# Query and key rows of an attention layer: turned by VectorE and a way through DRAM instead of by TensorE

## What is computed

```python
x = x + 0.5 * ffn(layernorm(x))
x = x + attn(layernorm(x))
x = x + 0.5 * ffn(layernorm(x))

# attn, 32 query heads, 8 key/value heads, 128 columns a head
q, k, v = x @ Wq.T, x @ Wk.T, x @ Wv.T           # split into heads
q, k = rmsnorm(q, q_norm_w), rmsnorm(k, k_norm_w)
scores = q @ k.T / sqrt(128) + alibi_and_causal_bias
out = softmax(scores) @ v                        # 4 query heads share a key/value head
return out @ Wo.T
```

## Time and profile before

| | us |
|---|---|
| median of 3 runs | 1220.47 (1220.09 to 1221.01) |
| span of the profiled execution | 1218.6 |
| one round of 8 units in attention (slots 29 to 36) | 92.85 |

### The profile page before, as it was taken

One profiled execution on the slowest core, in us unless ns is written; L12 is line 12 of the kernel. 1 busy time (PEld: TensorE's weight loads), 2 busy tenths in 40 slices (PEclk: granted clock), 3 DMA queues, 4 the chain that ended last, 5 costly groups with the idle time before them and its releaser, 6 DMA issues.

```text
span 1218.6 us, 18533 instructions
## 1 busy us (share of the span) xinstructions
PE 1206.2 (99%) x6368; PEld 1062.1 (87%) x6368; DVE 834.9 (69%) x2035; ACT 753.5 (62%) x1758; POOL 652.8 (54%) x526
## 2 busy tenths in 40 slices
PE   6999999999999999999999999999999999999999
PEld 5888888899998999999999999999999888888887
DVE  7876665776666577677677677667767878755555
ACT  4554442357677767767768767767767774544442
POOL 5796561635675625724824824823824343865550
DMA  6152222212213123122122122122122020221101
GB/s 235 42 175 94 103 105 104 94 47 87 79 44 104 44 79 103 39 84 96 44 87 89 50 87 87 53 79 96 53 78 87 20 68 9 71 69 53 52 18 69
DMA packets 33596, 93.77 MB, mean 77 GB/s; under 512 B 4128, under 2 KB 5056, under 8 KB 31456
## 3 DMA queue, kind: packets, MB, share of 16 engines
q1 hardware_dynamic: 33264, 92.29, 22.2%
q10 hardware_dynamic: 240, 0.30, 0.1%
HBM read 62.69 MB, written 29.88 MB: 76 GB/s over the span
## 4 chain that ended last, share of the span: by engine, by line
PE 98%; DVE 1%; DMA 0%; ACT 0%; SPq 0%; issue 0%
PE bank L369 22%; PE bank L367 22%; PE bank L368 21%; PE bank L674 6%; PE bank L479 4%; PE bank L473 4%; PE bank L474 4%; PE bank L688 3%; PE bank L693 3%; PE bank L689 3%; PE bank L619 2%; PE bank L395 1%; PE bank L655 1%; PE bank L622 1%; PE bank L383 1%; DMA x_rows<-x 0%
## 5 line engine op out<-in xcount | busy, mean ns | idle before, releaser
L1066 ACT ACTIVATE prob<-prob,neg_top 128x128 f32<-128x128 f32 (+3 forms) x256 | 141.2, 554 | 87.6 <-DVE neg_top L1517 56.9
L1817 POOL TENSOR_TENSOR rows<-rows,row_root_y 128x640 f32<-128x640 f32 x64 | 80.5, 1257 | 194.1 <-DVE row_root_y L1205 192.9
L1811 POOL TENSOR_TENSOR square<-rows 128x640 f32<-128x640 f32 x64 | 79.3, 1254 | 158.7 <-DVE rows L1560 131.1
L1686 POOL TENSOR_TENSOR w_l_late<-raw_late,w_h_late 128x512 fp32r<-128x512 f32 (+1 forms) x59 | 91.5, 1565 | 71.8 <-ACT w_h_late L809 71.8
L1075 ACT ACTIVATE prob<-prob,inverse 128x128 f32<-128x128 f32 (+3 forms) x252 | 121.1, 553 | 4.4 <-DVE inverse L1522 4.4
L1535 DVE TENSOR_TENSOR probT_l<-bank,probT_h 128x512 fp32r<-128x512 f32 x160 | 101.4, 683 | 28.5 <-ACT probT_h L1081 28.5
L1081 ACT CAST probT_h<-bank 128x512 fp32r<-128x512 f32 x160 | 84.6, 596 | 41.4 <-PE bank L674 41.4
L1281 DVE SCALAR_TENSOR_TENSOR x_rows<-bank,x_rows 128x512 f32<-128x512 f32 x111 | 74.8, 687 | 44.4 <-PE bank L479 44.4
L367 PE MATMUL bank<-o_h,oT_h 128*128 128x512 f32 x256 | 104.7, 409 | 0.0
L369 PE MATMUL bank<-o_h,oT_l 128*128 128x512 f32 x256 | 100.8, 394 | 0.0
L368 PE MATMUL bank<-o_l,oT_h 128*128 128x512 f32 x256 | 99.8, 390 | 0.0
(11 more groups left out here) (237 smaller groups left out, 3808.5 us busy)
## 6 DMA issues: line engine op xcount, KB each, us to landing
x_ring<-x_between SPq DMA_DIRECT2D x64, 256.0 KB, 2.6
x_between<-x_ring SPq DMA_DIRECT2D x56, 256.0 KB, 2.0
raw_late<-w_qkv SPq DMA_DIRECT2D x8, 1536.0 KB, 6.5
raw_early<-ffn_w SPq DMA_DIRECT2D x21, 512.0 KB, 4.1
scaled<-raw_early SPq DMA_DIRECT2D x21, 512.0 KB, 2.7
raw_late<-scaled SPq DMA_DIRECT2D x21, 512.0 KB, 3.7
raw_late<-w_o SPq DMA_DIRECT2D x8, 1024.0 KB, 5.0
x_between<-x_rows SPq DMA_DIRECT2D x8, 256.0 KB, 2.0
```

The source lines that it names most:

```text
L1066: last = act.activation(p, p, ACT.Exp, bias=neg_top[:, h:h + 1], scale=-1.0, accum_out=total[:, h:h + 1])
L1686: return pool.tensor_tensor(lo, raw, hi.bitcast(F32), ALU.subtract)
```

## The change

The rows of 54 units (list BLOCKED: 4 to 60 without 6, 10 and 14) no longer go through TensorE. As soon as GpSimd has normed them, VectorE transposes the 128x640 rows in 32x32 squares, SBUF to SBUF (`block_rows(n + 2)`): in odd slots behind the inversion of the sums (and behind oT_l), in even slots between the ring addition and probT_l. SP stores the squares in DRAM, where there are two rooms, and loads them back by four DMAs that put each square in its place (`store_rows`, `fetch_rows`). ScalarE and VectorE then make rounded parts and remainders from the SBUF tile turned_rows instead of from PSUM. The scale now goes to k instead of q. In the order of SP, the store and the four loads of unit n + 2 stand around ring_store and ring_load of the slot. Scores of such a unit wait for two new semaphores. The room for DMA descriptors of GpSimd is halved, to make room in SBUF.

```diff
+SQ = 32
+BLOCKED = tuple(n for n in range(4, UNITS - 3) if n % TB != 2 or n > 2 * B * TB)
+        row_blocks = sb("row_blocks", [P // SQ, G + 1, SQ])
+        turned_rows = sb("turned_rows", [P // SQ, G + 1, SQ])
+        def by_block(queries):
+            return queries[:, :, :].rearrange("p h (a t) -> p a h t", t=SQ)
@@ tensor: scores
+                if n in BLOCKED:
+                    pe.wait_ge(q_rest_done, blocked_nth(n) + 1)
+                    pe.wait_ge(k_rest_done, blocked_nth(n) + 1)
@@ tensor: slot
-                turn_rows(n + 1)
+                if n + 1 not in BLOCKED:
+                    turn_rows(n + 1)
@@ scalar: turn_rows
+                if n in BLOCKED:
+                    act.wait_ge(rows_back, 16 * (P // SQ) * (blocked_nth(n) + 1))
+                    act.copy(by_block(qT_h), turned_rows[:, :, 0:G, :]).then_inc(qT_hi_done, 1)
+                    act.activation(kT_h[:, t * P:(t + 1) * P].rearrange("p (a q) -> p a q", q=SQ), turned_rows[:, :, G, :], ACT.Copy,
+                                   scale=k_scale[:, g:g + 1]).then_inc(kT_hi_done, 1)
+                    return
@@ vector: turn_rows
+                if n in BLOCKED:
+                    dve.wait_ge(qT_hi_done, n + 1)
+                    dve.tensor_tensor(by_block(qT_l), turned_rows[:, :, 0:G, :], by_block(qT_h).bitcast(F32), ALU.subtract).then_inc(q_rest_done, 1)
+                    cols = slice(t * P, (t + 1) * P)
+                    dve.wait_ge(kT_hi_done, n + 1)
+                    dve.scalar_tensor_tensor(kT_l[:, cols].rearrange("p (a q) -> p a q", q=SQ), turned_rows[:, :, G, :], k_scale[:, g:g + 1],
+                                             kT_h[:, cols].bitcast(F32).rearrange("p (a q) -> p a q", q=SQ),
+                                             ALU.mult, ALU.subtract).then_inc(k_rest_done, 1)
+                    return
@@ vector
+            def block_rows(n):
+                dve.wait_ge(rows_normed, n + 1)
+                if blocked_nth(n):
+                    dve.wait_ge(rows_away, 16 * blocked_nth(n))
+                dve.transpose(row_blocks[:, :, :, :], rows[:, n % LEAD, 0:G + 1, :].rearrange("p h (b k) -> p b h k", k=SQ)).then_inc(rows_blocked, 1)
@@ vector: slot, ahead of turn_rows and add_products
+                if n % 2 and n + 2 in BLOCKED:
+                    block_rows(n + 2)
@@ vector: slot, behind project_out, ahead of turn_probabilities(n)
+                if n % 2 == 0 and n + 2 in BLOCKED:
+                    block_rows(n + 2)
@@ sync
+            def store_rows(n):
+                nth = blocked_nth(n)
+                if nth > 1:
+                    sp.wait_ge(rows_back, 16 * (P // SQ) * (nth - 1))
+                sp.wait_ge(rows_blocked, nth + 1)
+                sp.dma_start(row_turns[nth % 2], row_blocks[:, :, :, :].rearrange("p b h t -> p (b h t)")).then_inc(rows_away, 16)
+            def fetch_rows(n):
+                nth = blocked_nth(n)
+                away = row_turns[nth % 2]
+                if nth:
+                    sp.wait_ge(q_rest_done, nth)
+                    sp.wait_ge(k_rest_done, nth)
+                sp.wait_ge(rows_away, 16 * (nth + 1))
+                for b in range(P // SQ):
+                    sp.dma_start(turned_rows[b * SQ:(b + 1) * SQ, :, :, :].rearrange("k a h t -> k a (h t)"),
+                                 away.rearrange("(a k) (b c) -> b k a c", k=SQ, b=P // SQ)[b]).then_inc(rows_back, 16)
@@ sync: slot
+                blocked = n + 2 in BLOCKED
+                if blocked and n % 2:
+                    store_rows(n + 2)
                 if n:
                     ring_store(n - 1)
+                if blocked and n % 2:
+                    fetch_rows(n + 2)
+                elif blocked:
+                    store_rows(n + 2)
                 if n and n + 1 < UNITS:
                     ring_load(n + 1)
+                if blocked and n % 2 == 0:
+                    fetch_rows(n + 2)
```

More of the change, by code:

```diff
@@ L338, in keys_first, with blocked_nth @@
             return n >= UNITS - 2
+        def by_block(queries):
+            return queries[:, :, :].rearrange("p h (a t) -> p a h t", t=SQ)
+        def blocked_nth(n):
+            return BLOCKED.index(n)
         def tail(p, s, b, t):
@@ L716, in slot @@
                         project_out(n - 2)
-                    if n + 1 < UNITS:
+                    if n + 1 < UNITS and n + 1 not in BLOCKED:
                         turn_rows(n + 1)
@@ L1048, in turn_rows @@
                 act.wait_ge(full[r.bank], r.nth)
-                act.activation(qT_h[:, :, :], banks[r.bank][:, :].rearrange("p (h q) -> p h q", h=G), ACT.Copy,
-                               scale=q_scale[:, g:g + 1]).then_inc(qT_hi_done, 1)
+                act.copy(qT_h[:, :, :], banks[r.bank][:, :].rearrange("p (h q) -> p h q", h=G)).then_inc(qT_hi_done, 1)
                 if not keys_first(n):
@@ L1054, in turn_keys @@
             def turn_keys(n):
-                t = unit(n)[2]
+                g, _, t = unit(n)
                 r = results["turn_k", n]
                 act.wait_ge(full[r.bank], r.nth)
-                act.copy(kT_h[:, t * P:(t + 1) * P], banks[r.bank][:, 0:P]).then_inc(kT_hi_done, 1)
+                act.activation(kT_h[:, t * P:(t + 1) * P], banks[r.bank][:, 0:P], ACT.Copy, scale=k_scale[:, g:g + 1]).then_inc(kT_hi_done, 1)
             def exponentials(n, heads):
@@ L1483, in turn_rows @@
                 dve.wait_ge(qT_hi_done, n + 1)
-                dve.scalar_tensor_tensor(qT_l[:, :, :], banks[r.bank][:, :].rearrange("p (h q) -> p h q", h=G), q_scale[:, g:g + 1],
-                                         qT_h[:, :, :].bitcast(F32), ALU.mult, ALU.subtract).then_inc(evac[r.bank], 1)
+                dve.tensor_tensor(qT_l[:, :, :], banks[r.bank][:, :].rearrange("p (h q) -> p h q", h=G), qT_h[:, :, :].bitcast(F32),
+                                  ALU.subtract).then_inc(evac[r.bank], 1)
                 if not keys_first(n):
@@ L1493, in turn_keys @@
                 dve.wait_ge(kT_hi_done, n + 1)
-                dve.tensor_tensor(kT_l[:, cols], banks[r.bank][:, 0:P], kT_h[:, cols].bitcast(F32), ALU.subtract).then_inc(evac[r.bank], 1)
+                dve.scalar_tensor_tensor(kT_l[:, cols], banks[r.bank][:, 0:P], k_scale[:, g:g + 1], kT_h[:, cols].bitcast(F32),
+                                         ALU.mult, ALU.subtract).then_inc(evac[r.bank], 1)
+            def block_rows(n):
[3 more added lines that the diff above has]
+                dve.transpose(row_blocks[:, :, :, :], rows[:, n % LEAD, 0:G + 1, :].rearrange("p h (b k) -> p b h k", k=SQ)).then_inc(rows_blocked, 1)
             def scores(n):
@@ L2145 @@
     x_between = nc.dram_tensor("x_between", (B * TB, P, DM), F32, kind="Internal").ap()
-    build(nc, scaled, x_between, *args)
+    row_turns = nc.dram_tensor("row_turns", (2, P, (G + 1) * P), F32, kind="Internal").ap()
+    build(nc, scaled, x_between, row_turns, *args)
     return run_bass_kernel_spmd(nc, [arrays], core_ids=[0]).results[0]["y"]
```

31 lines of the change are left out of this document (17 added, 14 removed).

## The result

The changed kernel takes 1233.21 us, the median of 4 runs (1233.17 to 1234.51), against 1220.48 us for the kernel before on the same chip. The ratio is 1.0108, with a 95% interval of 1.0093 to 1.0122: slower by about 12.7 us. The profiled execution's span is 1231.9 us, against 1218.6 before.

A forecast was written before the change was run, and what follows sets the result against it. TensorE, busy 99%, was taken as the bound, with small margins behind it. Terms 11.9 (t=2), 5.4 (t=3), 2.8 (t=0), -1.7 (t=1), -3.8 (early) gave +14.6 on 1220.5: 1235 us; 8 in 10 range 1218 to 1252.

The forecast's parts named there:

- The lock in t=2: Slots with n mod 4 = 2: remainders with two SBUF operands wait for GpSimd's norm, delaying scores; +0.99 us a slot.
- The turn: VectorE's transpose of a unit's 128x640 rows: holds VectorE 0.74 us, bounds 0.62 and 1.48.
- The chain in t=3: Slots with n mod 4 = 3: late probT_l delays scores, exponentials, oT_l and the output projection; +0.45 us a slot.
- t=0: Slots with n mod 4 = 0: remainders wait for GpSimd's norm, kT_l delays the next scores; +0.23 us a slot.
- t=1: Slots with n mod 4 = 1: oT_l 0.28 us later, output projection still starts sooner; -0.15 us a slot.
- Early slots: Slots 3 to 11: seven lose TensorE's transposes and don't wait for oT_l; 0.54 us gained each, 3.8 in all.
- Remainders of t=3: qT_l and kT_l made in slots with n mod 4 = 3: over 3 us before kT_l is needed; cost nothing.
- without the lock: Rival: the remainders run through GpSimd's work as the PSUM ones do now; 1214.5 us, faster; chance 0.12.
- second remainder first: Rival: VectorE waits for GpSimd's norm, but its second remainder goes ahead of GpSimd's v_l; 1226 us; chance 0.12.
- long turn: Rival: VectorE's transpose of a unit's rows takes twice the length, 1.48 us; 1252 us; chance 0.13.
- slow DRAM: Rival: the rows' way through DRAM is too slow; at twice the latencies +29, 1264 us; chance 0.05.
- All 29 us kept: Rival: TensorE keeps the full gain of 54 units' transposes, needing oT_l 0.5 us earlier; 1191 us; chance 0.04.

The follow-up runs named there:

- first kernel of one part alone: Kernel before, with qT_l and kT_l of the 54 units made from an SBUF tile of zeros instead of PSUM, transposes kept; 1233.95 us, ratio 1.0117.

## Why the prediction was right

Forecast 1235 us, measured 1233.2. The steps, one by one:

- **The lock in t=2**, the largest term: forecast +0.99 a slot, measured +0.87. qT_l was forecast to end 0.55 us behind the norm, 11.56 us into the slot; it ends at 11.55. Mis-sized was kT_l: forecast 0.60 us behind qT_l, measured 0.46. Of GpSimd's first v_l I had added the whole 0.44 us behind qT_l, and it ends 0.31 behind it (769.26); kT_l ends 0.15 behind that, forecast 0.16. The Trainium skill (SBUF — State Buffer, section "SBUF: two separate sides"), by which such a VectorE operation and a GpSimd operation exclude each other for the whole instruction, agrees with the 1.50 us beside GpSimd and the 0.69 us without it.
- **The turn**: forecast to hold VectorE 0.74 us, measured 0.76 (835 ns, from its start to the next operation's 0.76). The reduction of the same 128x640 was the right row. The estimate of 1.55 us from the Trainium skill (VectorE: DVE Perf Modes, section "The three transpose paths") was twice too long: five times the figure for 128x128 in bf16 isn't what one instruction of 128x640 in float32 takes here. (By the sum's own steps it would also have given 1254 us, not 1252: 23 slots at 0.81 us.)
- **The chain in t=3**: probT_l forecast to start 1.18 us into slot 43, and it does (770.69 - 769.51); oT_l forecast to end at 7.82, measured 7.80; the slot +0.45, measured +0.38 to +0.45.
- **t=0**: forecast +0.23, measured +0.14, by the same step, kT_l; **t=1**: forecast -0.15, measured -0.21, as less comes in from t=0.
- **The waits**: forecast about 1 us for the remainders in t=2, about 1 for oT_l in t=3 and 0.4 in t=0. TensorE's weight loads wait 0.92, 1.05 and 0.50 us there (slots 42, 43 and 40).
- **Early slots**: forecast -0.54 each, measured -0.55 to -0.60.
- **Remainders of t=3**: forecast 0, measured 0, but by luck. The reason given, over 3 us until kT_l is needed, looks at the wrong reader: in the kernel without the units of t=3 the long kT_l made probT_l late, and the next slot lost some 0.46 us more. In the changed kernel the two operations happen to fall between two of GpSimd's.
- **DRAM, SP, ScalarE**: forecast 0, and the kernel with turn and DMAs unused is no slower than that with the turn alone. ScalarE's waits for the rows stay under the 2 us that would have spoken against it. A load took SP 0.43 us in the median, and up to 1.69, where I had used the 0.32 of the earlier trace rows; nothing hung on it.
- **Not forecast**: slot 13 (+2.20; the sum has nothing for it, since its rows' transposes stay) and slot 12 (+0.48). I had read slots 40 to 43 and taken their GpSimd for that of all slots. In slots 11 to 13 GpSimd is busy with squares and weights where it is idle in slots 41 and 43, and there the remainders of t=0 and the turn of an odd slot, costed at nothing, cost something.

The miss of 1.4 us in the sum (14.6 forecast, 13.2 measured) is in part luck, two larger ones against each other: 2.5 us too much for t=0, t=2 and t=3, against 1.7 too little for t=1 with its slot 13; early and late slots make the other 0.6. The rest of the 1.8 us between forecast and measurement is that the median lies 1.3 us above the profiled span, not 1.9.

Of the rivals, "without the lock" fell with the first kernel of one part alone, "second remainder first" with the order seen in slot 42 (the first v_l ends at 769.26, kT_l at 769.41), "long turn" and "slow DRAM" with their rows. "All 29 us kept" is bounded from two sides: with three of five transposes left out and nothing added, 12 us come back, of the 54 x 0.33 = 18 that are left out.

## What to carry to other kernels

Work that moves from a saturated engine to an idle one isn't free where a third engine shares something with the idle one: before the second operand of a VectorE operation moves from PSUM to SBUF, look for every operation of GpSimd that can run at that time, in every slot of a period and not in one. The gain of work taken from TensorE is no more than the smallest margin behind it (with three of five transposes left out, 0.05 to 0.15 us of 0.33 in two of four slots); read for each place when its next operand is ready. And a change that is good in some places and bad in others can be made in the good ones alone: 18 of 54 units gave 9 us where all 54 cost 13.

## What the runs showed of the hardware that I had not expected

- A VectorE operation with two SBUF operands stretches by what it meets, not by its size: kT_l, 128x128, took 0.34 us beside an idle GpSimd, 0.54 beside its remainders, 1.40 beside its squares (1.25 us each) and 1.92 beside operations of 1.85 us. It ends soon behind the operation that it met: qT_l 0.55 us behind the norm in slot 42 and behind the mixing in slot 12, kT_l 0.15 behind the squares in slot 11, both less than the 0.69 and 0.34 us that they take undisturbed. Whoever came first lost nothing: the norm took 1.26 us beside the waiting qT_l, as before. GpSimd's operations stretch when they come second: v_l's pair from 0.88 to 1.37 us.
- A turn of 128x640 in float32 in 32x32 squares took 827 to 846 ns, in all 54 cases, and no GpSimd operation lengthened it, nor it one of GpSimd's: the 1.85 us operation beside it in slot 42 took 1.86 before.
- TensorE's granted clock: in the kernel with the late output projection it waited 2.64 us in slot 41, and for the 3.75 us behind that the granted clock was 0.54, near the 1.2 GHz level: its products of 128x384 followed each other in 0.31 us, at full clock in 0.17. So that wait cost more than its own length. Not every such wait did: in slot 29 of the same kernel TensorE waited 2.76 us and the clock was 1.00 over the whole slot, while in slot 26 it was 0.51 for the 2.59 us behind a wait of only 1.88 us (600.53 to 602.41). In the changed kernel, where TensorE's products waited at most 0.73 us in attention, the clock over attention was 1.00.
